# Expert stage: the second half of the tokens is routed inside the first sweep over the experts

## The reference

```python
logits = xf @ gate_weight.T                       # 2048 x 32
scores = sigmoid(logits)
sfc = scores + e_score_correction_bias
group_scores = sfc.reshape(T, 8, 4).max(-1)       # best of each group
gmask = the 4 best groups;  masked = where(gmask, sfc, 0)
topk_idx = top_k(masked, 6)                       # 6 experts a token
tw = scores[topk_idx];  tw = tw / (tw.sum() + 1e-20) * 2.5
combine[token, expert] = tw                       # 2048 x 32, mostly zero
for each expert: acc += combine[:, e] * (silu(xf @ g.T) * (xf @ u.T) @ dn.T)
out = acc + shared expert                         # silu(x @ sg.T) * (x @ su.T) @ sd.T
```

## Time and profile before

| | |
|---|---|
| time, median of 3 runs | 1915.25 us (1915.21 to 1915.48) |
| the profiled execution's own time | 1916.08 us |
| its span | 1914.2 us |
| mean granted TensorE clock over the span | 0.951 of full speed |
| busy share of the span | PE 91%, weight loads 57%, DVE 73%, ACT 65%, POOL 30% |
| expert stage, from the first gate product to the last `down` | 756.8 to 940.6 us |

### The profile page before, as it was taken

One profiled execution on the slowest core, in us unless ns is written; L12 is line 12 of the kernel. 1 busy time (PEld: TensorE's weight loads), 2 busy tenths in 40 slices (PEclk: granted clock), 3 DMA queues, 4 the chain that ended last, 5 costly groups with the idle time before them and its releaser, 6 DMA issues. The chain is left out here.

```text
span 1914.2 us, 68172 instructions
## 1 busy us (share of the span) xinstructions
PE 1739.0 (91%) x29702; PEld 1098.4 (57%) x29724; DVE 1391.9 (73%) x2413; ACT 1244.9 (65%) x2174; POOL 579.3 (30%) x463
## 2 busy tenths in 40 slices
PE   7899999999989578699989999999999999847898
PEld 5477777777765265344446666666666665535443
DVE  2677777777753584677679889988988987356565
ACT  3377777777744283224268888888888888347243
POOL 4222222223130350466512222223223220033365
PEclk8899999999999788899979999999999999869999
DMA  4355555555500301365566556555655552040011
GB/s 158 94 140 138 150 144 145 140 141 151 125 11 0 66 4 35 102 172 138 139 106 104 96 106 103 99 106 100 103 105 97 101 93 28 1 69 4 28 45 39
DMA packets 67196, 178.40 MB, mean 93 GB/s; under 512 B 20532, under 2 KB 24756, under 8 KB 66484
## 3 DMA queue, kind: packets, MB, share of 16 engines
q1 hardware_dynamic: 64756, 170.85, 40.7%
q10 hardware_dynamic: 2144, 3.20, 0.7%
HBM read 84.39 MB, written 1.31 MB: 45 GB/s over the span
## 5 line engine op out<-in xcount | busy, mean ns | idle before, releaser
L734 ACT ACTIVATE Pb<-ps 128x512 f32<-128x512 f32 (+1 forms) x832 | 451.7, 597 | 50.1 <-PE ps L678 31.2
L701 PE MATMUL ps<-Pb,V 128*17 128x64 f32 (+1 forms) x13312 | 380.6, 248 | 0.7 <-ACT Pb L734 0.7
L813 DVE TENSOR_REDUCE MX<-ps 128x2 f32<-128x804 f32 (+1 forms) x384 | 364.1, 984 | 22.1 <-PE ps L642 20.8
L701 PEld LDWEIGHTS ps<-Pb,V 128*17 128x17 f32 (+1 forms) x13312 | 250.5, 97 | 87.2 <-issue 43.2
L815 DVE TENSOR_REDUCE MX<-ps 128x1 f32<-128x402 f32 (+1 forms) x512 | 266.0, 569 | 30.7 <-PE ps L646 24.7
L857 POOL TENSOR_TENSOR ABO<-CT 128x1601 bf16<-128x1601 f32 x43 | 123.0, 2861 | 532.7 <-DMA CT<-ctxT 532.7
L737 ACT ACTIVATE Pb<-ps 128x1024 f32<-128x1024 f32 (+1 forms) x224 | 204.6, 959 | 41.0 <-PE ps L682 38.3
L642 PE MATMUL ps<-KST,QW 50*128 50x402 bf16 (+1 forms) x1024 | 176.3, 340 | 12.8 <-issue 3.1
L678 PE MATMUL ps<-QW,KST 50*128 50x128 bf16 (+1 forms) x3328 | 165.6, 219 | 4.2 <-ACT Pb L734 2.4
L760 ACT ACTIVATE V<-ps 128x512 f32<-128x512 f32 (+1 forms) x256 | 129.3, 520 | 41.4 <-PE ps L582 34.2
L646 PE MATMUL ps<-KST,QW 96*128 96x402 bf16 (+1 forms) x512 | 148.8, 340 | 5.8 <-POOL QW L847 0.8
(11 more groups left out here) (271 smaller groups left out, 3166.8 us busy)
## 6 DMA issues: line engine op xcount, KB each, us to landing
CT<-ctxT SPq DMA_DIRECT2D x43, 800.5 KB, 4.7
KST<-HL SPq DMA_DIRECT2D x320, 100.1 KB, 3.0
KST<-C SPq DMA_DIRECT2D x320, 100.1 KB, 3.0
Pb<-routed SPq DMA_DIRECT2D x44, 256.0 KB, 4.0
ABO<-ctxT SPq DMA_DIRECT2D x10, 800.5 KB, 5.4
T<-ctxT SPq DMA_DIRECT2D x10, 800.5 KB, 4.3
KST<-HL SPq DMA_DIRECT2D x128, 50.0 KB, 2.7
KST<-C SPq DMA_DIRECT2D x128, 50.0 KB, 2.7
```

The lines of the kernel that those rows point to most:

```text
L701: mm = nc.tensor.matmul(ps[32 * quad:32 * quad + m, SUM, oc:oc + nh * S], V[0:n, b % 2, tile, v0:v0 + m], Pb[0:n, buffer(b, x), ti * att.W ...
L734: nc.scalar.activation(Pb[0:n, buffer(b, x), i * 512:(i + 1) * 512], score_bank(b, x, i)[0:n, :], ACT.Exp, scale=att.scale).then_inc(exps, 1)
L813: nc.vector.reduce_max(MX[:, b % 2, 2 * j:2 * j + 2], work(job)[:, :, 0:n], AX.X).then_inc(freed["dve"], 1)
```

## The change

- Tokens are routed in two halves of 1024 (8 tiles each), `tables(h)`; the tables lie in `V` in place of `ABO`. The logits of half h go to bank h, with a sigmoid for each half. The first half's products wait for chunks 0 and 1 alone.
- DVE does steps 0 to 4 of half 0 (up to the second search for the 8 largest), then item 0, then steps 5 to 7 of half 0. The eight steps of half 1 follow items i = 3 to 10 of sweep one, one step behind each.
- PE turns half 0 behind item i = 1 (before: all behind i = 0), so item 1's gate and up products stand ahead of the turn. It turns half 1 behind i = 12. Both use banks 6 and 7. `down` of item 0 waits for the second sigmoid in place of the turned banks.
- ACT copies two turned banks behind its i = 1 and two behind its i = 12.
- SP stores half 0 where it stored all; it stores half 1 and waits for it when it comes to the spread weights of sweep two's first item.
- ACT has a one-element sigmoid ahead of its waits.

```diff
             if role == "pe":
-                for c in range(NC):
-                    eng.wait_ge(ready[0], ready[1] + c)
-                for t in range(NT):
-                    mm = nc.tensor.matmul(ps[:, 0, t * E:(t + 1) * E], T[:, t * 128:(t + 1) * 128], w("gate"),
-                                          start=True, stop=True)
-                mm.then_inc(s["logit"], 1)
+                for h in range(2):
+                    for c in range(2 * h, 2 * h + 2):
+                        eng.wait_ge(ready[0], ready[1] + c)
+                    for t in range(NT):
+                        mm = nc.tensor.matmul(ps[:, h, t * E:(t + 1) * E], T[:, (h * NT + t) * 128:(h * NT + t + 1) * 128], w("gate"),
+                                              start=True, stop=True)
+                    mm.then_inc(s["logit"], 1)
             if role == "act":
-                eng.wait_ge(s["logit"], 1)
-                nc.scalar.activation(SC, ps[:, 0, :].rearrange("p (t e) -> p t e", t=NT), ACT.Sigmoid
-                                     ).then_inc(s["score"], 1)
+                nc.scalar.activation(WARM[:, :], epst[:, :], ACT.Sigmoid)
+                for h in range(2):
+                    eng.wait_ge(s["logit"], h + 1)
+                    SC = next(tables(h))
+                    nc.scalar.activation(SC, ps[:, h, 0:NT * E].rearrange("p (t e) -> p t e", t=NT), ACT.Sigmoid
+                                         ).then_inc(s["score"], 1)
...
+            def dve_route(h, step):
+
+                SC, SFC, GSC, GM8, GR, GM, MK, MK8, MR, TW, SM = tables(h)
+                if step == 0:
+                    eng.wait_ge(s["score"], h + 1)
+                    link(nc.vector.tensor_tensor(SFC, SC, w("gate_b").unsqueeze(1).broadcast_to([128, NT, E]), ALU.add))
...
+            def pe_turn(h):
+
+                TW = list(tables(h))[9]
+                eng.wait_ge(s["parts"], h + 1)
+                if h:
+                    eng.wait_ge(s["weights"], 2)
+                for k in range(2):
+                    for t in range(4):
+                        tr = nc.tensor.matmul(ps[0:E, 6 + k, t * 128:(t + 1) * 128], TW[:, 4 * k + t, :], w("ident"),
+                                              start=True, stop=True)
+                    tr.then_inc(s["turned"], 1)
+
+            def act_turned(h):
+                for k in range(2):
+                    eng.wait_ge(s["turned"], 2 * h + k + 1)
+                    nc.scalar.activation(ck(BYE, 2 * h + k), ps[0:E, 6 + k, :], ACT.Copy).then_inc(s["weights"], 1)
+
+            def sp_routed(h):
+
+                eng.wait_ge(s["weights"], 2 * h + 2)
+                eng.dma_start(ROUTED[:, h * 1024:(h + 1) * 1024], BYE[:, h * 1024:(h + 1) * 1024]).then_inc(stored, 16)
+                eng.wait_ge(stored, 16 * (h + 1))
...
+            TURN = 12
...
-                        eng.wait_ge(s["weights"], NC)
+                        eng.wait_ge(s["score"], 2)
...
-                    if i == 0:
-                        eng.wait_ge(s["parts"], 1)
...
+                    if i in (1, TURN):
+                        pe_turn(0 if i == 1 else 1)
...
             if role == "act":
-                for sweep, item in items:
+                for i, (sweep, item) in enumerate(items):
                     act_item(sweep, item)
+                    if i in (1, TURN):
+                        act_turned(0 if i == 1 else 1)
...
             if role == "dve":
+                for step in range(5):
+                    dve_route(0, step)
                 for i, (sweep, item) in enumerate(items):
                     dve_item(sweep, item)
+                    if i == 0:
+                        for step in range(5, 8):
+                            dve_route(0, step)
+                    if 3 <= i < 11:
+                        dve_route(1, i - 3)
...
-                eng.wait_ge(s["weights"], NC)
-                eng.dma_start(ROUTED, BYE).then_inc(stored, 16)
-                eng.wait_ge(stored, 16)
+                sp_routed(0)
                 sp_weights(*routed[0])
                 sp_weights(*routed[1])
                 for i, (sweep, item) in enumerate(routed):
+                    if i + 2 == NI - 1:
+                        sp_routed(1)
                     if i + 2 < len(routed):
                         sp_weights(*routed[i + 2])
```

More of the change, by code:

```diff
@@ L1678, in moe_stage, with link @@
[L1678 to L1681 removed]
+            chained = [0]
+            def link(ins, wait=True):
+                chained[0] += 1
+                ins.then_inc(s["chain"], 1)
+                if wait:
+                    eng.wait_ge(s["chain"], chained[0])
+            def dve_route(h, step):
[3 more added lines that the diff above has]
+                    link(nc.vector.tensor_tensor(SFC, SC, w("gate_b").unsqueeze(1).broadcast_to([128, NT, E]), ALU.add))
+                    link(nc.vector.memset(GSC[:, :, NG:12], BIG))
+                    link(nc.vector.memset(MK[:, :, E:34], BIG))
+                    link(nc.vector.reduce_max(GSC[:, :, 0:NG], SFC.rearrange("p t (g s) -> p t g s", g=NG), AX.X))
+                if step == 1:
+                    for t in range(NT):
+                        link(nc.vector.max(GM8[:, t, :], GSC[:, t, :]), t == NT - 1)
+                if step == 2:
+                    for t in range(NT):
+                        link(nc.vector.match_replace(GR[:, t, :], GM8[:, t, :], GSC[:, t, :], -BIG), t == NT - 1)
+                if step == 3:
+                    link(nc.vector.tensor_scalar(GM, GR[:, :, 0:NG], -BIG, None, ALU.is_equal))
+                    link(nc.vector.tensor_tensor(MK[:, :, 0:E].rearrange("p t (g s) -> p t g s", g=NG),
+                                                 SFC.rearrange("p t (g s) -> p t g s", g=NG),
+                                                 GM.unsqueeze(3).broadcast_to([128, NT, NG, GS]), ALU.mult))
+                    link(nc.vector.tensor_scalar(MK[:, :, 0:E], MK[:, :, 0:E], 0.0, None, ALU.add))
+                if step == 4:
+                    for t in range(NT):
+                        link(nc.vector.max(MK8[:, t, :], MK[:, t, :]), t == NT - 1)
+                if step == 5:
+                    for t in range(NT):
+                        link(nc.vector.match_replace(MR[:, t, :], MK8[:, t, :], MK[:, t, :], -BIG), t == NT - 1)
+                if step == 6:
+                    link(nc.vector.tensor_scalar(MR[:, :, 0:E], MR[:, :, 0:E], -BIG, None, ALU.is_equal))
+                    link(nc.vector.tensor_tensor(TW, SC, MR[:, :, 0:E], ALU.mult))
+                    link(nc.vector.reduce_sum(SM, TW, AX.X))
+                if step == 7:
+                    link(nc.vector.tensor_scalar(SM, SM, 1e-20, None, ALU.add))
+                    link(nc.vector.reciprocal(SM, SM))
+                    link(nc.vector.tensor_tensor(TW, TW, SM.unsqueeze(2).broadcast_to([128, NT, E]), ALU.mult))
+                    nc.vector.tensor_scalar(TW, TW, ROUTE_SCALE, None, ALU.mult).then_inc(s["parts"], 1)
```

66 lines of the change are left out of this document (7 added, 59 removed).

## The result

The changed kernel's median is 1908.64 us over 7 runs (1900.48 to 1917.39), that of the kernel before 1915.68 over 7 (1915.21 to 1925.55); the ratio is 0.9954, with a 95% interval of 0.9932 to 0.9977. The forecast was 1908.6, a ratio of 0.9965. So it is faster, by 6 to 9 us by the three ratios; their intervals reach from 3 to 13.

The account below looks back on a forecast made before the run. Serial routing, turn, store and spread were taken to bound the part ahead of the sweep, PE the sweep. -11.0 + 0.6 + 2.2 + 1.6 = -6.6 us from 1915.25 gave 1908.6 us; own range 1906.5 to 1911.3, wider range 1905.0 to 1913.5.

Parts of the forecast that it names:

- The new start: Routing, turn and store ahead of the sweep: half 0's store issued 11.0 us earlier; bounds 12.8 to 8.3.
- Restart: PE after waiting for item 1's spread: the clock falls in the idle, giving back 0.6 us; from 0 to 2.2.
- Half 1's steps: On DVE in items 3 to 10: 8.9 us more work overfills its list, giving back 2.2 us; from 0 to 4.
- rival C: DVE's SBUF operations in the sweep kept out for all of POOL's time: +1.9 us, 1917.2; chance 0.07.
- Half 1's turn: On PE behind item 12, where PE bounds the sweep: gives back 1.6 us; from 1.2 to 3.3.
- At nothing: Costs put at zero: second store on SP, one-element sigmoid on ACT, tables in `V`, the shared expert's `down` without its wait.
- A: DVE does not bind in the sweep; waits for POOL fall away and slack takes the rest: -8.8 us, 1906.4; chance 0.20.
- B: The clock takes it: both turns at half speed, restart twice as long: -1.6 us, 1913.6; chance 0.12.
- D: The change does nothing, since something counted as serial was hidden: 1915 us; chance 0.05.
- signs of being wrong: DVE's item 0 waiting past 767, sweep steps well over 1.1 us each, or SP's second store holding up weights.

Follow-up runs that it names:

- again: The changed kernel measured once more, nothing edited; median 1907.62 us, ratio 0.9970 to the kernel before.
- in_wait: Against the changed kernel, half 1's eight steps moved into DVE's wait for the first spread weights, at item 1; median 1903.51 us, ratio 0.9943.
- in_wait_keep: As in_wait, plus 26 products that nobody reads in PE's wait for the first spread weights; median 1906.37 us, ratio 0.9960.
- all_in_wait: Against the changed kernel, half 1's steps in DVE's wait, 22 unread products and half 1's turn in PE's; median 1905.44 us, ratio 0.9946.
- no_half1: Changed kernel without half 1's routing, turn and two copies, storing the first half's weights twice; median 1902.84 us, ratio 0.9940.

## Why the prediction was right, by its own steps

The forecast was -6.6 us; inside the stage it was -7.4, -7.6 and -7.6. The mechanism was the forecast one: half of the routing taken off the path to the first spread weights, and part of it paid back by the restart, by half 1's steps and by its turn. But one wait was not where the forecast had it, and the start gained 2.1 us more than forecast while restart and steps gave back up to 1.4 more. That these cancel to 1 us is partly luck.

- **The new start: -11.0 forecast, -13.06 measured, 0.3 outside its own bounds.** DVE was through item 0 at 11.4 behind the mark where I had 12.7. I had DVE wait for the shared expert's silus, with steps 0 to 4 (5.2 us) hidden ahead of that wait. The silus were earlier, and the steps took 7.0 us under POOL's hold, a collision for which this term had nothing. DVE's own list then set the start: item 0 was done at 11.4 both in the profiled execution, where half of the shared products ran at half speed, and in `again`, where all ran at full speed. Only in `in_wait` and `in_wait_keep`, where the clock was at half until 10.6, was the wait the forecast one:

```profile
766.90 0.69 DVE L1800 TENSOR_TENSOR Pb<-ps,Pb 128x512 f32<-128x512 f32 x1 [0.70 <-ACT Pb L1790]
```

  There item 0 was done at 12.7, as forecast. The turn took 0.3 more than 1.64. The store took 1.95 in place of 2.58, and the landing 4.67 in place of 5.06. I had kept 2.58 for a store of half the bytes. By the Trainium skill, "DMA: Bandwidth & Descriptors", section "Anatomy of one DMA — SWDGE (gpsimd) path", the estimate was 0.3 less; the trace has 0.63 less. That section is on transfers that GpSimd issues, and this store is issued by SP. A late clock gives what in_wait had: 26.73, 0.2 over the 26.5 that the forecast's 11.0 means.
- **Restart: +0.6 forecast, within 0 to 2.2; +1.6 in the profiled execution, +0.8 in the two others.** The clock fell 1 to 2.6 us before the end of 6.4 us of idle, and stayed at half for 6.8 us in all three, where I had 3.4 and the double only as a bound. The four executions with products in the wait show it as the cause: 6.97 or 6.98 each, at a full clock.
- **Half 1's steps: +2.2 forecast; 1.6 to 3.7 measured, 2.6 between the means.** DVE bound items 3 to 10, as worked out (35.07 busy of 37.31). They took 4.3 us more than before, not the 2 of "about 35"; PE's slack came back only behind item 11, where this kernel took 24.88 to 25.40 against 26.45 without the steps. The collisions were too low in my sum: +0.7 for all. The changed kernel's step 3 in the sweep,

```profile
808.82 0.18 DVE L1661 TENSOR_SCALAR V<-V 128x64 f32<-128x64 f32 x1
809.04 1.26 DVE L1662 TENSOR_TENSOR V<-V 128x256 f32<-128x256 f32 x1
810.34 0.80 DVE L1665 TENSOR_SCALAR V<-V 128x256 f32<-128x256 f32 x1
```

and the same step in all_in_wait, where POOL stood still:

```profile
774.75 0.20 DVE L1661 TENSOR_SCALAR V<-V 128x64 f32<-128x64 f32 x1
774.98 0.42 DVE L1662 TENSOR_TENSOR V<-V 128x256 f32<-128x256 f32 x1
...
775.44 0.29 DVE L1665 TENSOR_SCALAR V<-V 128x256 f32<-128x256 f32 x1
```

  2.32 us against 0.98. Steps 6 and 7 went from 1.21 and 1.19 to 1.9 and 2.3. Well over 1.1 us for a step was one of my signs of being wrong, and it came for these three. That is 3.2 us of collisions, of which the items' own operations gave back half: the eight items less their steps needed about 25.2 us of DVE, not 26.9. The lock of rival C is real for these forms, as the Trainium skill, "SBUF — State Buffer", section "SBUF: two separate sides" has it for two inputs or a two-port mode; L1656 and L1668, with one input, were not slowed. L1665 has one input too and was slowed; that it ran in such a mode no run here shows. But C needed 1.55 us of it in every item. The steps lost 3.2 us in three items, and L1806 lost 2.9 us in all eight (its time over 16 times 0.69), together 0.8 an item.
- **Half 1's turn, with its copies: +1.6 forecast, +1.45 measured** (26.45 in three runs against 25.02; 26.96 in in_wait_keep).
- **At nothing:** the second store, the copies, the one-element sigmoid: no_half1 agrees for the store; the copies are inside the turn's 1.45, and no run shows the sigmoid alone.
- **Rivals.** A (DVE does not bind) is refuted by the 37.31. B's parts are real: a turn at half speed, in part or whole, in six variants, and a restart of twice the forecast length in all three executions of the changed kernel. But never all three came together; the last turn was at full speed each time. C and D did not come.
- **What I did not foresee** is the size of the scatter outside the stage: one execution of each kernel would have given the wrong sign.

## What to carry to other kernels

Look for the wait that a transfer leaves on the engine that does the postponed work: the eight steps cost 2.6 us in a list that is nearly full and none where DVE sat idle for 8.7. When an operation is moved on one engine, move what consumes it on the others in the same step; moved on PE alone, the turn held up the store by 6.2 us, and with ACT's copies by 1.5. Before a wait is called hidden, look whether the engine was idle at its end: here DVE was not. When a transfer lands late twice in the same way, look in the DMA view for a load of instructions beside it. Where runs scatter by more than the effect, compare the stretch between two fixed marks in several executions, not the whole.

## What the runs showed of the hardware

- Up to the store the stage repeats to 0.02 us: 17.84 to 17.86 in seven executions, with the shared products at full speed or at half until 8 us behind the mark, since DVE bound there. A half clock that reached further, into item 1's products or the turn, made the store 1.35 to 2.15 us later (19.19 to 19.99).
- 26 unread products in a wait of PE kept the clock full: 1.00 from 774.30 to 787.19, against 0.63 over 7.77 us without them.
- A DVE operation with two SBUF inputs, 0.42 us alone, took 1.26 and 1.31 beside POOL's operations, and a TENSOR_SCALAR of 0.29 took 0.80 and 1.13; MAX8 did not change (0.66 to 0.68).
- A load of 16 KB of instructions beside a transfer went with one of its 16 shares ending 1.3 to 1.6 us late, and so with the landing: 6.1 and 6.3 us against 4.7 for the spread weights, 3.24 against 1.95 for the store. It was so in all three executions in which such a load fell into one of these transfers.
